# Late key steps, one VectorE order and two waits for constants moved in a three-stage transformer kernel

## The chip, the cores and the metric

The kernel runs on one core of one Trainium2 chip. Its time is the device time of one execution in microseconds (us); the kernel before took 1489.43 us (median of 3 runs, 1488.98 to 1492.85). One execution was profiled, and all rows below come from it.

## The reference

The input is 16 sequences (batches) of 256 tokens with 128 channels. The result is a chain of residual blocks, all in float32:

```python
x = x + 0.5 * channel_mix(layernorm(x))                 # L0 ffn
x = x + causal_attention(layernorm(x))                  # L0 attn, 16 heads of width 8
x = x + 0.5 * channel_mix(layernorm(x))
x = x + 0.5 * experts(layernorm(x))                     # L1 ffn: top 2 of 8 experts
x = x + focus_attention(layernorm(x))                   # L1 attn
x = x + 0.5 * experts(layernorm(x))
```

The focus attention is iterated three times over the same keys and values:

```python
q = (ln(x) @ Wq.T + bq) * sc                            # per head below
k, v = ln(ln(x)) @ Wk.T, ln(ln(x)) @ Wv.T + bv
for i in range(3):
    sq, sk = ln(q @ lq.T + lq_b), ln(k @ lk.T + lk_b)
    out = softmax(window(sq @ sk.T)) @ (v @ lv.T + lv_b)
    q = q + out                                         # unless converged
output = out @ Wo.T + bo
```

## The kernel before, in words

Every engine has its own program, written out by hand in the order in which it shall run; semaphores join the programs. The stages are: the causal stage with the channel mixes; the expert mixture by groups of two batches (`mixture`), some of it dense and some by sorted tiles; the focus stage (`fast_focus`, three iterations over 16 batches, so 48 rounds); the second expert mixture.

The keys, queries and values of the focus stage are made by group as well. For groups 0 to 4 this is done within the mixture; for groups 5, 6 and 7 it is put into the first 13 rounds of iteration 0 and called *late* (`late_keys`, `KEYS_LATE`). A late group takes five steps, 0 to 4, in five rounds in a row: rounds 0 to 4 for group 5, 4 to 8 for group 6, 8 to 12 for group 7. So rounds 1, 5, 9 have step 1; rounds 2, 6, 10 have step 2; rounds 3, 7, 11 have step 3; rounds 0, 4, 8 have step 0 and rounds 4, 8, 12 step 4.

A round on TensorE is eight turns hp = 0 to 7. Each starts with the scores of two heads (`pair_scores`, L2145; S0 to S7 below). Between them stand:

- `fast_values(n, p, g)` (L2156, V0 to V3): exponentials times values for four heads, V0 to V2 of the round itself, V3 of the round before;
- `back_tokens` (L1633, ps_m<-ident,o_sb; BT0 and BT1): the transposes of the last round's result, both into one half of `ps_m`. BT1 waits until VectorE has read BT0's result (`normalise`, L3131 and L3138);
- `front_tokens`, `front_product`, `front_heads` (FT; FP, L2128; FH, ps_m<-ident,y x2): the queries of the round after next;
- the late work, which uses the same half of `ps_m` as BT0 and BT1: `key_tokens` (KT, step 1, ps_m<-ident,y x4), products L2022 of `key_queries` and `key_keys` (step 2) and `key_values` (step 3), and `key_heads` (step 3). Before BT0 of a late round TensorE waits for semaphore `K_read` or `K_hi`, which says that VectorE has read the last product.

VectorE's round, as the code has it:

```python
front_tokens, evacuate_group(n - 1, 3), front_deviations      # L3096, L3119, L3026/L3029/L3032
normalise(n - 1, 0), evacuate_group(n, 0), normalise(n - 1, 1)
front_heads, change                                           # L2923/L2932, L3147
evacuate_group(n, 1), front_parts, evacuate_group(n, 2)       # L3119, L3111/L3112, L3119
```

`front_deviations` ends in `hvar` (L3032), from which ScalarE makes the scale of the queries. The late steps stand between these: `key_norm2` (four L2540, step 1; TensorE's `key_tokens` waits for it), `key_queries` (L2898, step 2) and `key_values` (L2913, step 3).

ScalarE does the exponentials (L1420), eight to a round. The operands `q_st` and `k_st` of round n are written by DMA during round n - 1, from the parts that `front_parts` and GpSimd made in round n - 2.

Between the causal stage and the mixture every engine jumps over a long branch that isn't taken (`redo_causal`). GpSimd then makes eight constants (L957 to L964 and a select, L773) for `positions` and `tile_experts`, which run in group 1 of the mixture, about 50 us later.

Of the kernel before, what the change touches and what calls it, by code (L numbers as in the profile page):

```python
# [17 lines left out]
B, T, C = 16, 256, 128  # L18
# [50 lines left out]
def macaron_kernel(nc, a, out):  # L69
    ctx = ExitStack()  # L70
    with ctx:
# [1557 lines left out]
        def _(pe):  # L1629
# [562 lines left out]
            def fast_focus():  # L2192

                last_group(lambda g, u: mixture(g, u, 0, True, True, more=lambda g, e: ahead(0, g, e)))
                for it in range(MAX_ITER):
                    final = it == MAX_ITER - 1

                    def body(n, b, p, half):
# [4 lines left out]
                        for hp in range(HP):  # L2203
                            pair_scores(n, p, half, hp)
                            for g, step in late:
                                if (step, hp) == (2, 1):
                                    key_queries(g)
                                if (step, hp) == (3, 1):
                                    key_values(g)
                            if hp == 0 and again:  # L2210
                                for t in range(NT):
                                    back_tokens(n - 1, B - 1, it - 1, t)
                            if hp == 1 and again:
                                pe.wait_ge(sem("fast_o_read"), (n - 1 + B) * NT + NT + 1)
                            if hp == 3 and again:
                                change_sum(it - 1, 1)
                                front_product(ahead[0])
                            if hp == 1 and final and isinstance(b, int) and b == B - 1:
                                mix_tokens(FIRST)
                            if hp == 1:  # L2220
                                if ahead:
                                    front_tokens(ahead[0])
                                if not first:
                                    fast_values(n - 1, 1 - p, NGV - 1)
                            elif hp == 2 and ahead and not again:
                                front_product(ahead[0])
                            elif hp == 3:
                                if first and not it:
                                    pe.wait_ge(sem("M_comb"), FIRST * EXP + QUADS + 2)
                                if late:  # L2230
                                    fast_values(n, p, 0)
                                for g, step in late:
                                    if step == 1:
                                        pe.wait_ge(sem("K_hi"), g + 1)
                                    if step == 2:
                                        pe.wait_ge(sem("K_read"), g * 3 + 1)
                                    if step == 3:
                                        pe.wait_ge(sem("K_read"), g * 3 + 3)
                                    if step == 4:
                                        pe.wait_ge(sem("K_hi"), g + 2)  # L2240
                                if not first:
                                    back_tokens(n - 1, b - 1, it, 0)
                                if not late:
                                    fast_values(n, p, 0)
                            elif hp == 4 and not first:
                                back_tokens(n - 1, b - 1, it, 1)
                            elif hp == 5:
                                fast_values(n, p, 1)
                            elif hp == 6:
                                if ahead:  # L2250
                                    front_heads(ahead[0])
                                for g, step in late:
                                    if step in (2, 3):
                                        pe.wait_ge(sem("fast_o_read"), (n - 1 + B) * NT + NT + 1)
                                    if step == 2:
                                        key_keys(g)
                                    if step == 3:
                                        key_heads(g)
                                if not first and final:
                                    back_out(b - 1)  # L2260
                                if final and isinstance(b, int) and b == B - 1:
                                    mix_logits(FIRST, 0)
                            elif hp == 7:
                                if not first and final:
                                    back_project(b - 1)
                                fast_values(n, p, 2)
                                for g, step in late:
                                    if step == 1:
                                        pe.wait_ge(sem("fast_o_read"), (n - 1 + B) * NT + NT + 1)
                                        key_tokens(g)  # L2270

                    fast_steps(pe, it, body)
                    n = it * B + B - 1
# [167 lines left out]
            def ahead(k, g, e):  # L2441
# [7 lines left out]
                if (g, e) == (0, 7):  # L2449
                    mix_logits(a + 1, 0)  # L2450
                if (g, e) == (1, 1):
                    pe.wait_ge(sem("consts"), CONSTS + 8)
                    positions(k)
                if (g, e) == (2, 6):
                    quad_rows(k, 0)
# [12 lines left out]
            def tiles(k):  # L2468
# [6 lines left out]
                for c in CHUNKS[k]:  # L2475
                    for i in range(SLOTS):
# [11 lines left out]
                            tile_hidden(c + 1, i + 3 - SLOTS)  # L2488
                        tile_out(c, i, at[order_in(c) * SLOTS + i])

            for g in range(AHEAD):
                mixture(g, g % 2, 0, True, more=lambda g, e: ahead(0, g, e))
            pe.wait_ge(sem("tile_in_0"), 16)
# [11 lines left out]
        def _(dve):  # L2505
# [664 lines left out]
            def fast_focus():  # L3170
# [3 lines left out]
                for it in range(MAX_ITER):  # L3174
                    final = it == MAX_ITER - 1

                    def body(n, b, p, half):
# [7 lines left out]
                            front_tokens(ahead[0])  # L3185
                        if not first:
                            evacuate_group(n - 1, NGV - 1)
                        for g, step in late:
                            if step == 2:
                                key_queries(g)  # L3190
                            if step == 3:
                                key_values(g)
                        if ahead:
                            front_deviations(ahead[0])
                        for g, step in late:
                            if step == 0:
                                key_stats1(g)
                        if not first:
                            normalise(n - 1, it, 0)
                        evacuate_group(n, 0)  # L3200
# [4 lines left out]
                            front_heads(ahead[0], it + 1 if later else it)  # L3205
                        if not first:
                            change(n - 1, b - 1, it)
                        for g, step in late:
                            if step == 1:
                                key_norm2(g)  # L3210
                        evacuate_group(n, 1)
                        if not first and final:
                            back_out(b - 1)
                        for g, step in late:
                            if step == 0:
                                key_norm1(g)
                        if ahead:
                            front_parts(ahead[0], p)
                        for g, step in late:
# [350 lines left out]
            def ahead(k, g, e):  # L3570
# [10 lines left out]
                if (g, e) == (0, 7):  # L3581
                    mix_ranks(a + 1)
                if (g, e) == (1, 1):
                    dve.wait_ge(sem("consts"), CONSTS + 8)
                    tile_experts(k)
                if (g, e) == (2, 5):
                    if k:
# [35 lines left out]
            def weigh_tiles(k):  # L3623
# [14 lines left out]
                quad_out(CHUNKS[k][-1], QUADS - 2)  # L3638
                quad_out(CHUNKS[k][-1], QUADS - 1)

            for g in range(AHEAD):
                mixture(g, g % 2, 0, True, more=lambda g, e: ahead(0, g, e))
            weigh_tiles(0)
# [44 lines left out]
```

## Time and profile before

| | before |
|---|---|
| median of 3 runs | 1489.43 us |
| the profiled execution | 1489.43 us, span 1487.7 us |
| TensorE busy, matmuls | 1326.3 us, 89% of the span |
| VectorE busy | 1008.0 us, 68% |
| ScalarE busy | 866.1 us, 58% |
| GpSimd busy | 529.1 us, 36% |
| mean granted TensorE clock | 0.967 of full speed |

Iteration 0 of the focus stage runs from 681.56 us (first exponential) to 884.43 us. In the rows, PE is TensorE, PEld its weight load, DVE VectorE, ACT ScalarE and POOL GpSimd. A fp32 matmul has two records, so an x16 in the trace is eight matmuls in the code.

### The profile page before, as it was taken

The numbers are of one execution on the slowest core, as the hardware profiler recorded it, in microseconds if no ns is written. First come the engines' busy times: TensorE is split into PE (matmuls) and PEld (weight loads), VectorE is DVE, ScalarE is ACT, GpSimd is POOL, SyncE is SP. The second block draws the span as 40 slices with busy tenths as digits, with TensorE's granted clock in tenths as the row PEclk, the third lists the DMA queues.
The fourth block names the chain that finished last, engine by engine and source line by source line (L and its number), as shares of the span: only waits on it lengthen the run. The fifth ranks groups of instructions, "written<-read, shape, count | busy, mean of one in ns | idle before, by whom it ended". The sixth has DMA issues, their size and how long they took to land. (4 is left out here: it accounts for less than half of the span.)

```text
span 1487.7 us, 36643 instructions
## 1 busy us (share of the span) xinstructions
PE 1326.3 (89%) x11651; PEld 919.3 (62%) x11651; DVE 1008.0 (68%) x3275; ACT 866.1 (58%) x1613; POOL 529.1 (36%) x818
## 2 busy tenths in 40 slices
PE   4799999998769999998889989999899999799998
PEld 2566666666546787775555545555555555567876
DVE  3688889888738755776676666665766666576544
ACT  3567777776424444435667767777666666333453
POOL 5366666665310503112323332333322222003444
PEclk9799999999869999999999999999999999999999
DMA  5332232233040112005454454455444443001232
GB/s 142 85 81 57 77 85 56 70 85 86 1 129 1 40 52 64 20 12 123 105 128 114 118 131 109 114 128 131 113 103 114 111 113 82 2 10 49 84 120 78
DMA packets 81070, 123.64 MB, mean 83 GB/s; under 512 B 10124, under 2 KB 64676, under 8 KB 71722
## 3 DMA queue, kind: packets, MB, share of 16 engines
q1 hardware_dynamic: 77866, 115.71, 30.5%
q0 software_dynamic: 3072, 6.30, 1.4%
q8 instruction: 68, 1.11, 0.3%
q14 instruction: 64, 0.52, 0.1%
HBM read 88.28 MB, written 33.56 MB: 82 GB/s over the span
## 5 line engine op out<-in xcount | busy, mean ns | idle before, releaser
L1420 ACT ACTIVATE e_buf<-ps_q 128x1024 f32<-128x1024 f32 x192 | 196.5, 1023 | 96.3 <-PE ps_q L2145 95.9
L2156 PE MATMUL ps_o<-e_buf,v_st 128*32 128x256 f32 x3072 | 210.0, 392 | 4.6 <-POOL v_st L1025 4.2
L1420 ACT ACTIVATE e_buf<-ps_k 128x1024 f32<-128x1024 f32 x192 | 195.7, 1019 | 20.3 <-PE ps_k L2145 18.2
L2006 PEld LDWEIGHTS ps_o<-w,e_buf 128*128 128x128 f32 x1280 | 152.4, 193 | 13.1 <-issue 12.0
L2006 PE MATMUL ps_o<-w,e_buf 128*128 128x128 f32 x1280 | 158.7, 278 | 0.0
L2594 DVE TENSOR_REDUCE mx<-ps_q 128x3 f32<-128x384 f32 x256 | 130.2, 548 | 27.4 <-PE ps_q L1710 26.8
L3119 DVE COPY o_sb<-ps_o 128x256 f32<-128x256 f32 x192 | 80.7, 421 | 100.2 <-PE ps_o L2156 60.7
L2145 PE MATMUL ps_q<-q_st,k_st 73*128 73x256 bf16 x768 | 119.6, 279 | 17.4 <-DMA q_st<-scr_q 15.4
L1237 ACT ACTIVATE e_buf<-ps_k 128x768 f32<-128x768 f32 x128 | 103.3, 807 | 47.9 <-PE ps_k L1721 45.9
L2156 PEld LDWEIGHTS ps_o<-e_buf,v_st 128*32 128x32 f32 x3072 | 81.3, 110 | 75.7 <-issue 36.4
L2145 PEld LDWEIGHTS ps_q<-q_st,k_st 73*128 73x128 bf16 x768 | 61.6, 99 | 97.7 <-issue 68.9
L2145 PE MATMUL ps_k<-q_st,k_st 73*128 73x256 bf16 x768 | 117.8, 276 | 1.9 <-ACT e_buf L1420 0.8
L886 POOL TENSOR_SCALAR_AFFINE_SELECT e_buf<-e_buf 128x512 f32<-128x512 f32 x128 | 85.5, 668 | 92.6 <-ACT e_buf L1237 91.0
L1336 ACT ACTIVATE e_buf<-ps_q,b_t 128x512 f32<-128x512 f32 x80 | 54.6, 685 | 93.3 <-PE ps_q L1998 89.6
L1336 ACT ACTIVATE e_buf<-ps_k,b_t 128x512 f32<-128x512 f32 x80 | 53.9, 685 | 71.9 <-PE ps_k L1998 68.7
L1633 PE MATMUL ps_m<-ident,o_sb 128*128 128x128 f32 x508 | 80.3, 281 | 12.9 <-DVE o_tok L3138 8.3
L2145 PEld LDWEIGHTS ps_k<-q_st,k_st 73*128 73x128 bf16 x768 | 72.8, 99 | 18.4 <-ACT e_buf L1420 10.3
L1047 POOL COPY heads_out<-o_tok 128x256 f32<-128x256 f32 (+1 forms) x32 | 12.9, 402 | 197.3 <-DVE dsum L3153 99.7
L1033 POOL TENSOR_TENSOR rest<-qk,parts 128x256 f32<-128x256 f32 x48 | 32.6, 680 | 139.1 <-DVE parts L3112 139.0
L1707 PE MATMUL ps_q<-mask_q,ident_b 128*128 128x256 bf16 x256 | 72.5, 283 | 9.5 <-DVEq L3415 4.5
L984 POOL DMA_INDIRECT slots_in<-heads_out,vp_all x40 | 39.3, 983 | 103.1 <-DVEq L3513 91.7
L1633 PEld LDWEIGHTS ps_m<-ident,o_sb 128*128 128x128 f32 x508 | 57.3, 142 | 30.0 <-DVE o_tok L3138 17.8
(403 smaller groups left out, 3068.0 us busy)
## 6 DMA issues: line engine op xcount, KB each, us to landing
q_st<-scr_q SPq DMA_DIRECT2D x64, 576.0 KB
k_st<-scr_k SPq DMA_DIRECT2D x192, 192.0 KB
scr_q<-parts SPq DMA_DIRECT2D x64, 192.0 KB, 2.1
scr_k<-parts SPq DMA_DIRECT2D x72, 64.0 KB
slots_in<-heads_out SPq DMA_DIRECT2D x3, 1536.0 KB
slots_out<-heads_out SPq DMA_DIRECT2D x18, 256.0 KB, 2.0
heads_out<-slots_in SPq DMA_DIRECT2D x15, 256.0 KB
out_dram<-x SPq DMA_DIRECT2D x8, 256.0 KB
```

The lines of the kernel that those rows point to most:

```text
L886: pool.affine_select(out=e, in_=e, compare_op=ALU.is_ge, fill=0.0, base=0, pattern=[[0, 2], [0, 2], [1, P]], channel_multiplier=-1)\
L984: pool.indirect_dma_start(slots_in[c], bass.IndirectOffsetOnAxis(ap=slot_no[c][:, k, t:t + 1], axis=0), normed_rows(ND + c * 2 + t // GT)[ ...
L1237: act.activation(e_buf[g % 2][:, hp * 2 % HG:hp * 2 % HG + 2, 0:3 * P], ps_k[:, :, 0:3 * P], ACT.Exp, bias=SHIFT).then_inc(sem("fast_exp"), 1)
L1336: act.activation(h_sb[e % 2][:, f, :], bank, ACT.Relu, bias=b1_t[:, j:j + 1])\
L1420: act.activation(e_buf[g % 2][:, hp * 2 % HG:hp * 2 % HG + 2, :], (ps_q, ps_k)[hp % 2][:, :, :], ACT.Exp).then_inc(sem("fast_exp"), 1)
L1633: return pe.transpose(dst, src, ident[0:k, 0:k])
L1707: mm(o[:, P:3 * P], ident_b[:, :], mask_q[:, :], start=True, stop=False, skip_group_check=True)
L2006: last = mm(ps_o[:, e % 2, t * P:(t + 1) * P], h_sb[e % 2][:, f, t * P:(t + 1) * P], w2[:, e * NF + f, :], start=f == 0, stop=f == NF - 1)
L2145: last = mm(bank[:, u, t * T:(t + 1) * T], k_st[p][0:ROWS_P1, hp * 2 + u, t * P:(t + 1) * P], q_st[p][0:ROWS_P1, hp * 2 + u, :], start=Tru ...
L2156: last = mm(ps_o[VW * j:VW * j + VW, g % 2, 0:T], v_st[p][:, kt, HG * g + j, :], e_buf[g % 2][:, j, kt * T:(kt + 1) * T], start=kt == 0, s ...
L2594: red(mx[:, h, :], ps_q[:, u, 0:3 * P].rearrange("p (c k) -> p c k", c=3), AX.X, ALU.max)\
L3119: dve.tensor_copy(o_sb[:, g, :], ps_o[:, g % 2, 0:T]).then_inc(sem("fast_evac"), 1)
```

## The change

There are four edits. On TensorE, in the 12 late rounds 1 to 12, V0 comes behind BT0 instead of ahead of it (so V0 comes behind the wait for `K_read` or `K_hi` too). On TensorE, `key_tokens` of step 1 moves from the end of the round (behind V2) to turn 6, ahead of S7 and V2. On VectorE, `key_queries` and `key_values` move behind `front_deviations`, and `key_norm2` behind the evacuation of V1. On TensorE and VectorE, the wait for the constants moves from group 1 of the mixture to the front of group 0. ScalarE, GpSimd and the DMA queue have the same program as before.

```diff
@@ TensorE, fast_focus
                             elif hp == 3:
                                 if first and not it:
                                     pe.wait_ge(sem("M_comb"), FIRST * EXP + QUADS + 2)
-                                if late:
-                                    fast_values(n, p, 0)
                                 for g, step in late:
...
                                 if not first:
                                     back_tokens(n - 1, b - 1, it, 0)
-                                if not late:
-                                    fast_values(n, p, 0)
+                                fast_values(n, p, 0)
...
                                 if ahead:
                                     front_heads(ahead[0])
                                 for g, step in late:
-                                    if step in (2, 3):
+                                    if step in (1, 2, 3):
                                         pe.wait_ge(sem("fast_o_read"), (n - 1 + B) * NT + NT + 1)
+                                    if step == 1:
+                                        key_tokens(g)
...
                                 fast_values(n, p, 2)
-                                for g, step in late:
-                                    if step == 1:
-                                        pe.wait_ge(sem("fast_o_read"), (n - 1 + B) * NT + NT + 1)
-                                        key_tokens(g)
@@ TensorE (VectorE alike, with tile_experts)
                 if (g, e) == (1, 1):
-                    pe.wait_ge(sem("consts"), CONSTS + 8)
                     positions(k)
...
+            pe.wait_ge(sem("consts"), CONSTS + 8)
             for g in range(AHEAD):
                 mixture(g, g % 2, 0, True, more=lambda g, e: ahead(0, g, e))
@@ VectorE, fast_focus
                             evacuate_group(n - 1, NGV - 1)
-                        for g, step in late:
-                            if step == 2:
-                                key_queries(g)
-                            if step == 3:
-                                key_values(g)
                         if ahead:
                             front_deviations(ahead[0])
                         for g, step in late:
                             if step == 0:
                                 key_stats1(g)
+                        for g, step in late:
+                            if step == 2:
+                                key_queries(g)
+                        for g, step in late:
+                            if step == 3:
+                                key_values(g)
...
                             change(n - 1, b - 1, it)
-                        for g, step in late:
-                            if step == 1:
-                                key_norm2(g)
                         evacuate_group(n, 1)
...
                         for g, step in late:
                             if step == 0:
                                 key_norm1(g)
+                        for g, step in late:
+                            if step == 1:
+                                key_norm2(g)
```

TensorE in round 1, from S6 to the first scores of round 2. Before, the transposes of `y` by four (KT) are the last of the round:

```order
L2145 MATMUL ps_q<-q_st,k_st 128x256 x4
L1633 MATMUL ps_m<-ident,y 128x128 x2
L2145 MATMUL ps_k<-q_st,k_st 128x256 x4
L2156 MATMUL ps_o<-e_buf,v_st 32x256 x8
L1633 MATMUL ps_m<-ident,y 128x128 x4
L2145 MATMUL ps_q<-q_st,k_st 128x256 x4
```

Now FH and KT stand together (two and four transposes, x6), ahead of S7 and V2:

```order
L2145 MATMUL ps_q<-q_st,k_st 128x256 x4
L1633 MATMUL ps_m<-ident,y 128x128 x6
L2145 MATMUL ps_k<-q_st,k_st 128x256 x4
L2156 MATMUL ps_o<-e_buf,v_st 32x256 x8
L2145 MATMUL ps_q<-q_st,k_st 128x256 x4
```

What moved is KT: S7 and V2 are now queued behind whatever KT waits for.

TensorE in round 2, from FP (L2128) to BT1. Before, V0 (L2156) follows S3:

```order
L2128 MATMUL ps_m<-block_w,y_t 128x128 x2
L2145 MATMUL ps_k<-q_st,k_st 128x256 x4
L2156 MATMUL ps_o<-e_buf,v_st 32x256 x8
L1633 MATMUL ps_m<-ident,o_sb 128x128 x4
L2145 MATMUL ps_q<-q_st,k_st 128x256 x4
L1633 MATMUL ps_m<-ident,o_sb 128x128 x4
```

Now BT0 (the first L1633) does:

```order
L2128 MATMUL ps_m<-block_w,y_t 128x128 x2
L2145 MATMUL ps_k<-q_st,k_st 128x256 x4
L1633 MATMUL ps_m<-ident,o_sb 128x128 x4
L2156 MATMUL ps_o<-e_buf,v_st 32x256 x8
L2145 MATMUL ps_q<-q_st,k_st 128x256 x4
L1633 MATMUL ps_m<-ident,o_sb 128x128 x4
```

V0 and BT0 have changed places, with BT0's wait for `K_read` now ahead of both.

VectorE in rounds 1 and 2, from `dsum` of round 1 to the reciprocal of round 2, before (the line numbers of VectorE are five higher here than in the changed kernel):

```order
L3147 TENSOR_REDUCE dsum<-o_tok 128x1
L2540 TENSOR_SCALAR y<-y,mv_k,rstd_k 128x128 x4
L3119 COPY o_sb<-ps_o 128x256
L3111 COPY qk<-ps_m 128x256
L3112 CAST parts<-ps_m 128x256
L3119 COPY o_sb<-ps_o 128x256
L3096 COPY y_t<-ps_m 128x256
L3119 COPY o_sb<-ps_o 128x256
L2898 SCALAR_TENSOR_TENSOR qcur<-ps_m,rows 128x512
L3026 TENSOR_TENSOR cen<-ps_m,rows 128x256
L3029 TENSOR_TENSOR sqr<-cen 128x256
L3032 TENSOR_REDUCE hvar<-sqr 128x32
```

and now:

```order
L3142 TENSOR_REDUCE dsum<-o_tok 128x1
L3114 COPY o_sb<-ps_o 128x256
L2535 TENSOR_SCALAR y<-y,mv_k,rstd_k 128x128 x4
L3106 COPY qk<-ps_m 128x256
L3107 CAST parts<-ps_m 128x256
L3114 COPY o_sb<-ps_o 128x256
L3091 COPY y_t<-ps_m 128x256
L3114 COPY o_sb<-ps_o 128x256
L3021 TENSOR_TENSOR cen<-ps_m,rows 128x256
L3024 TENSOR_TENSOR sqr<-cen 128x256
L3027 TENSOR_REDUCE hvar<-sqr 128x32
L2893 SCALAR_TENSOR_TENSOR qcur<-ps_m,rows 128x512
```

`key_norm2` (the four TENSOR_SCALAR) is behind the copy of V1, and `key_queries` (`qcur<-ps_m`) behind the three instructions that end in `hvar`. `key_values` moved in the same way in step 3.

## Rows read from the trace of the kernel before

**Rows 1.** The page, busy us, share of the span and instructions of each engine:

```profile
PE 1326.3 (89%) x11651; PEld 919.3 (62%) x11651; DVE 1008.0 (68%) x3275; ACT 866.1 (58%) x1613; POOL 529.1 (36%) x818
```

**Rows 2.** Waits of TensorE, 681 to 890 us: total us, times, longest:

```profile
PE ps_m L1633 <- DVE o_tok L3138: 6.3, 13, 1.3
PE ps_q L2145 <- DMA q_st<-scr_q: 5.8, 4, 2.9
```

**Rows 3.** Timeline of TensorE, round 14, not late (start, us, instruction [idle before]):

```profile
851.67 0.60 PE L2145 MATMUL ps_k<-q_st,k_st 73*128 73x256 bf16 x4
852.11 0.60 PE L1633 MATMUL ps_m<-ident,o_sb 128*128 128x128 f32 x4
...
854.09 0.60 PE L1633 MATMUL ps_m<-ident,o_sb 128*128 128x128 f32 x4
...
856.86 0.44 PE L1633 MATMUL ps_m<-ident,y 128*128 128x128 f32 x2
```

**Rows 4.** Timeline of TensorE: rounds 6 and 8 in one row each, round 9:

```profile
760.59 0.60 PE L2145 MATMUL ps_q<-q_st,k_st 73*128 73x256 bf16 x4 [0.97 <-DMA q_st<-scr_q]
...
794.45 0.65 PE L1633 MATMUL ps_m<-ident,o_sb 128*128 128x128 f32 x4 [1.32 <-DVE o_tok L3138]
...
802.53 0.60 PE L2145 MATMUL ps_k<-q_st,k_st 73*128 73x256 bf16 x4
...
805.50 0.66 PE L1633 MATMUL ps_m<-ident,o_sb 128*128 128x128 f32 x4 [0.34 <-DVE o_tok L3138]
...
808.32 0.44 PE L1633 MATMUL ps_m<-ident,y 128*128 128x128 f32 x2 [0.19 <-DVE y L2932]
...
810.22 0.63 PE L1633 MATMUL ps_m<-ident,y 128*128 128x128 f32 x4
811.09 0.60 PE L2145 MATMUL ps_q<-q_st,k_st 73*128 73x256 bf16 x4 [0.24 <-DMA q_st<-scr_q]
```

**Rows 5.** Timeline of VectorE, round 9:

```profile
808.43 1.68 DVE L2540 TENSOR_SCALAR y<-y,mv_k,rstd_k 128x128 f32<-128x128 f32 x4
810.04 0.41 DVE L3119 COPY o_sb<-ps_o 128x256 f32<-128x256 f32 x1
```

**Rows 6.** Timeline of TensorE, round 10:

```profile
815.06 0.60 PE L2145 MATMUL ps_k<-q_st,k_st 73*128 73x256 bf16 x4
...
816.59 0.66 PE L1633 MATMUL ps_m<-ident,o_sb 128*128 128x128 f32 x4
...
818.02 0.66 PE L1633 MATMUL ps_m<-ident,o_sb 128*128 128x128 f32 x4 [0.34 <-DVE o_tok L3138]
```

**Rows 7.** Timeline of VectorE, round 10:

```profile
814.75 0.68 DVE L2898 SCALAR_TENSOR_TENSOR qcur<-ps_m,rows 128x512 f32<-128x512 f32 x1
815.35 0.41 DVE L3026 TENSOR_TENSOR cen<-ps_m,rows 128x256 f32<-128x256 f32 x1
...
816.37 0.42 DVE L3032 TENSOR_REDUCE hvar<-sqr 128x32 f32<-128x256 f32 x1
```

**Rows 8.** Timeline of TensorE, round 11:

```profile
829.31 0.71 PE L2128 MATMUL ps_m<-block_w,y_t 128*128 128x128 f32 x4 [0.78 <-DVE y_t L3096]
829.86 0.60 PE L2145 MATMUL ps_k<-q_st,k_st 73*128 73x256 bf16 x4
...
832.82 0.66 PE L1633 MATMUL ps_m<-ident,o_sb 128*128 128x128 f32 x4 [0.34 <-DVE o_tok L3138]
```

**Rows 9.** Timelines of TensorE, GpSimd and VectorE where the mixture starts:

```profile
425.33 2.08 PE L1998 MATMUL ps_q<-z_t,w 128*128 128x512 f32 x2 [3.46 <-issue]
...
426.85 0.29 POOL L773 TENSOR_SCALAR_AFFINE_SELECT k_const<-k_const 128x128 bf16<-128x128 bf16 x1
...
427.89 0.87 DVE L2531 BATCH_NORM_STATS2 st<-x 128x6 f32<-128x128 f32 x4 [4.76 <-issue]
...
428.44 2.08 PE L1998 MATMUL ps_q<-z_t,w 128*128 128x512 f32 x2 [1.04 <-ACT e_buf L1336]
```

**Rows 10.** Windows in round 3: length, busy us (x) by engine, PEclk, DMA:

```profile
727.00:730.40 3.40, 3.40 (x25) 1.65 (x23) 1.15 (x3) 1.37 (x3) 0.00 (x0) 0.51 0.60 135
```

More of the change, by code:

```diff
@@ L3583, in ahead @@
                 if (g, e) == (1, 1):
-                    dve.wait_ge(sem("consts"), CONSTS + 8)
                     tile_experts(k)
@@ L3639, in weigh_tiles @@
                 quad_out(CHUNKS[k][-1], QUADS - 1)
+            dve.wait_ge(sem("consts"), CONSTS + 8)
             for g in range(AHEAD):
```

## The prediction

> **What bounds the kernel now.** I read the page's engine line first: TensorE's matmuls are busy 89% of the span and no other engine is over 68% [rows 1], so wherever TensorE stops, the stop shows in the time unless something behind it waits anyway. Then the waits of TensorE over iteration 0 of the focus stage: 13 waits for `o_tok` (6.3 us) and 4 for the query operands (5.8 us) [rows 2]. Last the timelines, round by round. In a round that isn't late, S3 starts at 851.67, BT0 at 852.11, BT1 at 854.09 without a wait, FH at 856.86 [rows 3]: BT0 comes 0.44 behind S3, BT1 2.42 behind S3 (1.98 behind BT0, since V0 and S4 lie between), FH 2.77 behind BT1. In late round 9 V0 lies ahead of BT0, so only S4 lies between BT0 and BT1, and BT1 waits 0.34 for VectorE: S3 to BT1 is 2.97, to FH 5.79 instead of 5.19 [rows 3, 4]. TensorE is the pace of a late round, and VectorE is the engine that it waits for. Times below are starts.
>
> **V0 behind BT0, taken alone.** It gives a late round the order of rows 3: BT1 0.55 earlier. That holds only where VectorE has by then read the late product and `normalise` isn't held up. In rounds 4 and 8 BT1 waits 1.32 for `o_tok` [rows 4], because VectorE does `key_stats1` ahead of `normalise`; VectorE's own chain sets BT1 and the new order gives nothing. Round 0 has no BT0. In round 12 up to 0.6 could be won, but round 14 waits for its query operands (the second of the four waits in size, 5.8 - 2.9 - 0.97 - 0.24 = 1.7 [rows 2, 4]), which I expect to swallow it: 0, with -0.6 as the other end.
>
> **Step 1 (rounds 1, 5, 9): KT ahead of S7 and V2.** KT needs `key_norm2`, which is now behind VectorE's copy of V1. In round 9 as it was: BT1 805.50, `key_norm2` 808.43 to 810.11 (2.93 behind BT1), the copy behind it 0.41, KT 810.22 [rows 4, 5]. Now BT1 is at 802.53 + 2.42 = 804.95; the copy comes first, at 807.88, `key_norm2` starts about 0.35 later, 808.25, lasts 1.68, KT at 810.04. TensorE is free for it behind FH, at 807.72 + 0.3 = 808.0, so it stands still for 2.0, and S7 and V2 stand behind it. Before, S7 and V2 ran in that time: from FH to KT is 1.90, less 0.3 for FH itself 1.6, of which I take 1.5 for the two. KT itself takes 0.46 before the next may start. So the next S0 is at 810.04 + 0.46 + 1.5 = 812.0, against 811.09: +0.9. In round 10 a wait of 0.24 for `q_st` was swallowed on the way, in round 6 one of 0.97 [rows 4], in round 2 none: +0.9, +0.2 and +1.2, together **+2.3**. The ends: 0 if `key_norm2` ran before FH, which no row speaks for, and 3 x 2.0 = 6.0 if the whole standstill counts.
>
> The 1.68 are four operations of 128 columns in fp32, SBUF to SBUF, at a time when GpSimd copies and adds. Of that the Trainium skill ("GPSIMD Engine Reference", Key points) says that GpSimd shares its SBUF interfaces with VectorE, so that they contend. By that rule the 0.35 of delay would move `key_norm2` partly out of GpSimd's way and step 1 would cost some tenths less; the sum stays with the measured 1.68.
>
> **Step 2 (rounds 2, 6, 10): BT0 waits for `key_queries`, which is now behind `hvar`.** As it was: `key_queries` 814.75 to 815.43, over before TensorE had finished V0; BT0 816.59 [rows 6, 7]. Now `cen` takes its place; it needs FP and can start between 814.75 and 815.35, I take 815.25. `hvar` starts 1.02 later [rows 7], 816.27, `key_queries` 0.33 behind it, 816.6, and ends at 817.28; BT0 at 817.34. V0 is queued behind BT0, so nothing covers the wait of 817.34 - (815.06 + 0.44) = 1.84. BT1 follows 1.98 later, 819.32, against 818.02: **+1.3** in each, **+3.9**. From BT1 to the end of the round the order is as it was, and VectorE's and ScalarE's work for the next round hangs on the same TensorE instructions, so all of it shifts.
>
> **Step 3 (rounds 3, 7, 11): the same with `key_values`.** FP at 829.31 lasts 0.71; `cen` can start at 829.95, `hvar` at 830.97, `key_values` (128x512 as in rows 7, 0.68) ends at 831.98, BT0 at 832.04, BT1 834.02 against 832.82 [rows 8]: **+1.2** each, **+3.6**. Both ends for steps 2 and 3: -0.55 each if VectorE's read were over in time (the pure gain of the order), and +1.8 each if no part of V0 covered.
>
> **The wait for the constants.** GpSimd's last constant ends at 427.14, TensorE's first product of the mixture started at 425.33 and VectorE's first operation at 427.89 [rows 9]. VectorE loses nothing. TensorE starts up to 1.9 later; but its second product stood back by 1.04, and both gaps are of issue and not of data that the mixture needs, so that the later start may close one: between +0.8 and +1.9, I take **+1.0**. The wait that goes from group 1 was long met there: 0.
>
> **The clock.** Sum so far 2.3 + 3.9 + 3.6 + 1.0 = 10.8. In round 3, behind waits of which none is over 0.78 (round 11 has the same, [rows 8]), the granted clock is 0.51, the lower level of 1.2 GHz, for 3.4 us with TensorE busy all the time [rows 10]: up to 1.7 lost. Rounds 7 and 11 have the same waits and keep 2.4 GHz. The nine longer standstills give such falls more places. I put one more of them, **+1.5**, into the sum; the ends are -1.7 (the one in round 3 goes) and three or four more.
> The Trainium skill ("TensorE: Matmul & The Clock Gate", A second HAM failure mode: psum-queue depth-cycling) says that frequent short idles between groups of matmuls are enough to make the clock swing between its two levels. By that rule this change, which adds such idles, costs more than their length; the fall in round 3 agrees, rounds 7 and 11 show that it isn't certain.
>
> **Sum.** +12.3 on a profiled execution of 1489.43, which is also the median: **1501.7**. No later stage has a fixed time that could take the delay up; all the rest is queued behind TensorE.
>
> **Rivals.**
> *The clock falls in most of the standstills (slower still).* In five of the nine: 10.8 + 5 x 1.6 = 18.8, 1508.2. For it: round 3. Against it: the waits of 1.32 in rounds 4 and 8 [rows 4] had no such fall. The page's rule above would make this the likely case.
> *The new order wins (faster).* The mechanism is the earlier BT0: if VectorE's read of the late product ends before S3 + 0.44 in steps 2 and 3, and `key_norm2` before FH in step 1, ten rounds win 0.55 each, with +1.0 for the constants: -4.5, 1484.9. It decides at 815.5 in round 10; I have the read ending at 817.28 there. For it speaks only that rounds 13 to 15 run so.
> *No change.* The round is set by the query operands, and the standstills only replace waits for them. All four such waits are 5.8, of them the largest 2.9, and 0.97 and 0.24 are in the sum [rows 2, 4]; the remaining 1.7 is that of round 14, behind the late rounds. If VectorE's read comes about 1 earlier than I have it (`key_queries` in the gap ahead of `cen`), steps 2 and 3 come out near +0.3 and the total near +2: 1491.5.
>
> **How the numbers follow.** Forecast (10.8 with none to two more falls of the clock) 0.66, with a range of its own from 1496 to 1505; clock rival 0.13, no change 0.12, faster 0.09. A difference under 0.3% (4.5 us) can't be told from none here. Faster than 1485.0: 0.08; within: 0.13; slower than 1493.9: 0.79. The range that leaves out 2 in 10: 1493 to 1508.
>
> **What would show it.** In the changed kernel's timeline of TensorE: KT waits about 2.0 for `y` (L2535) in rounds 1, 5 and 9; BT0 waits about 1.8 for `qcur` in rounds 2, 6, 10 and about 1.7 for `vp_all` in rounds 3, 7, 11 (S3 to BT0 2.2 to 2.3); rounds 4 and 8 keep the wait of 1.3 for `o_tok`; S3 to BT1 in round 12 is 2.4. The first product of the mixture starts behind the last constant. Rounds of iterations 1 and 2 keep their lengths. I am wrong if BT0 shows no wait in steps 2 and 3, if the start of the focus stage moves by more than 2 us, or if rounds 1 to 12 together grow by less than 6 us.

## The result: 1.45% slower, and the profile after

| | before | after |
|---|---|---|
| median | 1489.2 us (4 runs, 1487.99 to 1492.85) | 1510.01 us (4 runs, 1505.88 to 1515.52) |
| ratio | | 1.0145, 95% interval 1.0116 to 1.0175 |
| span of the profiled execution | 1487.7 us | 1508.3 us |
| first exponential of the focus stage | 681.56 | 681.56 |
| iteration 0 of the focus stage | 202.9 us | 223.8 us |
| iteration 1 | 184.1 us | 183.9 us |

The forecast was 1501.7 with a range to 1508: the side was right, the size short by 8.3 us, and the time lies above the range. All of the loss is in iteration 0. The page's engine line after, beside [rows 1]:

```profile
PE 1336.4 (89%) x11651; PEld 927.8 (62%) x11651; DVE 1009.1 (67%) x3275; ACT 865.0 (57%) x1613; POOL 528.6 (35%) x818
```

No instruction was added, yet the matmuls are busy for 10.1 us more. That is the first hint: waiting alone would leave the busy time as it was.

The length of a round, from one first exponential (L1420) to the next, in both traces:

| round | step | before | after | grown by | I had |
|---|---|---|---|---|---|
| 1, 5, 9 | 1 | 13.50, 12.71, 12.00 | 14.74, 12.79, 12.78 | 2.1 | 2.3 |
| 2, 6, 10 | 2 | 15.16, 15.08, 15.08 | 16.41, 16.40, 16.40 | 3.9 | 3.9 |
| 3, 7, 11 | 3 | 13.51, 12.02, 12.01 | 17.22, 17.32, 17.39 | 14.4 | 3.6 |
| 4, 8 | 4 and 0 | 11.40, 11.40 | 11.40, 11.39 | 0.0 | 0 |
| 12 | 4 | 10.41 | 10.18 | -0.2 | 0 |
| 0, 13 | 0, none | 13.44, 11.90 | 13.85, 12.32 | 0.8 | 0 |

The waits of TensorE from 681 to 905 us after, the counterpart of [rows 2]:

```profile
PE ps_q L2145 <- DMA q_st<-scr_q: 5.4, 2, 3.3
PE ps_m L1633 <- DVE vp_all L2908: 5.1, 3, 1.7
PE ps_m L1633 <- issue: 5.1, 3, 1.7
PE ps_m L1633 <- DVE qcur L2893: 5.1, 3, 1.7
...
PE ps_m L1633 <- DVE o_tok L3133: 2.7, 2, 1.4
```

Each of the three predicted standstills is there three times, 1.7 long: `vp_all` is BT0 in step 3, `qcur` BT0 in step 2, and "issue" KT in step 1 (the view names no engine; KT starts 0.10 behind the end of VectorE's four instructions). The thirteen waits for `o_tok` have become two, those of rounds 4 and 8.

Step 1, TensorE in round 9 after, the counterpart of [rows 4]; then VectorE, of [rows 5]:

```profile
815.82 0.60 PE L2145 MATMUL ps_k<-q_st,k_st 73*128 73x256 bf16 x4
816.26 0.60 PE L1633 MATMUL ps_m<-ident,o_sb 128*128 128x128 f32 x4
...
818.24 0.60 PE L1633 MATMUL ps_m<-ident,o_sb 128*128 128x128 f32 x4
...
821.01 0.44 PE L1633 MATMUL ps_m<-ident,y 128*128 128x128 f32 x2
823.15 0.63 PE L1633 MATMUL ps_m<-ident,y 128*128 128x128 f32 x4 [1.70 <-issue]
```

```profile
821.12 0.42 DVE L3114 COPY o_sb<-ps_o 128x256 f32<-128x256 f32 x1
821.45 1.60 DVE L2535 TENSOR_SCALAR y<-y,mv_k,rstd_k 128x128 f32<-128x128 f32 x4
```

S3 to BT0 0.44, to BT1 2.42, to FH 5.19, as in a round that isn't late; then KT stands until `key_norm2` ends at 823.05.

Step 3, TensorE in round 11 after, the counterpart of [rows 8]:

```profile
844.71 0.71 PE L2128 MATMUL ps_m<-block_w,y_t 128*128 128x128 f32 x4 [0.77 <-DVE y_t L3091]
845.26 0.60 PE L2145 MATMUL ps_k<-q_st,k_st 73*128 73x256 bf16 x4
847.56 1.11 PE L1633 MATMUL ps_m<-ident,o_sb 128*128 128x128 f32 x4 [1.70 <-DVE vp_all L2908]
848.61 1.94 PE L2156 MATMUL ps_o<-e_buf,v_st 128*32 128x256 f32 x16
...
851.30 1.06 PE L1633 MATMUL ps_m<-ident,o_sb 128*128 128x128 f32 x4
...
853.14 1.94 PE L2156 MATMUL ps_o<-e_buf,v_st 128*32 128x256 f32 x16
...
857.67 1.07 PE L2156 MATMUL ps_o<-e_buf,v_st 128*32 128x256 f32 x16
```

The wait is what I had. What I had not is behind it: V0 and V1 take 1.94 instead of the 1.07 of V2. The windows say why (length, busy us and count of PE, PEld, DVE, ACT, POOL, then the granted clock, the DMA share and GB/s):

```profile
843.80:847.20 3.40, 1.28 (x10) 0.83 (x8) 2.74 (x9) 1.52 (x3) 0.00 (x0) 0.96 0.72 181
847.20:850.60 3.40, 3.04 (x21) 1.44 (x22) 0.85 (x3) 1.14 (x2) 0.00 (x0) 0.50 0.05 14
850.60:854.00 3.40, 3.40 (x20) 2.16 (x22) 1.44 (x5) 1.77 (x2) 0.00 (x0) 0.50 0.02 5
854.00:857.40 3.40, 3.40 (x25) 2.31 (x18) 1.89 (x6) 1.30 (x2) 1.08 (x2) 0.54 0.00 0
857.40:860.80 3.40, 3.40 (x46) 1.84 (x43) 0.86 (x3) 3.02 (x5) 2.68 (x4) 1.00 0.08 26
```

In the first window TensorE is busy for only 1.28 of 3.4 us. At its end, at 846.9, the clock falls to its lower level, 1.2 GHz, and it stays there for 10.2 us although TensorE is busy for nearly all of that time. Rounds 3 and 7 show the same, so rounds 2 to 11 have 30.7 us at the lower level. Before, they had 3.4 us, in round 3 [rows 10]. (A further fall of 6.8 us, across rounds 0 and 1, is in both traces.)

The start of the mixture after, the counterpart of [rows 9], TensorE and GpSimd:

```profile
426.30 0.29 POOL L773 TENSOR_SCALAR_AFFINE_SELECT k_const<-k_const 128x128 bf16<-128x128 bf16 x1
426.64 3.78 PE L1998 MATMUL ps_q<-z_t,w 128*128 128x512 f32 x4 [5.32 <-POOL k_const L773]
430.21 2.01 PE L1998 MATMUL ps_k<-z_t,w 128*128 128x512 f32 x4
432.07 0.60 PE L1633 MATMUL ps_m<-ident,rank 128*8 128x128 f32 x4
```

The first product waits for the last constant, but the gap of 1.04 ahead of the second is gone, and the focus stage starts at the same 681.56. That equality is partly chance: the changed kernel came to the constants 0.55 earlier (426.30 against 426.85), and its first `ps_m<-ident,rank` 1.50 earlier (432.07 against 433.57), since the clock rose at 430.5 instead of 433.4; by the start of the focus stage this was used up again, in a stretch where the change only takes out a wait that was long met.

### The profile page after: what moved, and what is told of

It is laid out like the page before. It is cut to its first block and busy times, and to the rows that moved or that the text cites. A ratio compares the mean times of both kernels' runs of the same rounds, so it can differ in the third digit from the quotient of the medians.

```text
span 1508.3 us, 36640 instructions
## 1 busy us (share of the span) xinstructions
PE 1336.4 (89%) x11651; PEld 927.8 (62%) x11651; DVE 1009.1 (67%) x3275; ACT 865.0 (57%) x1613; POOL 528.6 (35%) x818
## 5 line engine op out<-in xcount | busy, mean ns | idle before, releaser
L1420 ACT ACTIVATE e_buf<-ps_q 128x1024 f32<-128x1024 f32 x192 | 196.3, 1022 | 110.7 <-PE ps_q L2145 110.0
L2156 PE MATMUL ps_o<-e_buf,v_st 128*32 128x256 f32 x3072 | 214.8, 399 | 4.6 <-POOL v_st L1025 4.2
L1420 ACT ACTIVATE e_buf<-ps_k 128x1024 f32<-128x1024 f32 x192 | 195.6, 1019 | 28.2 <-PE ps_k L2145 27.3
L2145 PE MATMUL ps_q<-q_st,k_st 73*128 73x256 bf16 x768 | 122.1, 283 | 14.7 <-DMA q_st<-scr_q 12.6
L2156 PEld LDWEIGHTS ps_o<-e_buf,v_st 128*32 128x32 f32 x3072 | 82.4, 112 | 78.0 <-issue 38.9
L1633 PE MATMUL ps_m<-ident,o_sb 128*128 128x128 f32 x508 | 82.5, 287 | 19.7 <-DVE o_tok L3133 5.2
L1047 POOL COPY heads_out<-o_tok 128x256 f32<-128x256 f32 (+1 forms) x32 | 12.8, 400 | 209.9 <-DVE dsum L3142 108.5
L1633 PEld LDWEIGHTS ps_m<-ident,o_sb 128*128 128x128 f32 x508 | 60.2, 146 | 31.0 <-DVE o_tok L3133 12.2
```

What stands on the lines that cost most here:

```text
L1420: act.activation(e_buf[g % 2][:, hp * 2 % HG:hp * 2 % HG + 2, :], (ps_q, ps_k)[hp % 2][:, :, :], ACT.Exp).then_inc(sem("fast_exp"), 1)
L1633: return pe.transpose(dst, src, ident[0:k, 0:k])
L2145: last = mm(bank[:, u, t * T:(t + 1) * T], k_st[p][0:ROWS_P1, hp * 2 + u, t * P:(t + 1) * P], q_st[p][0:ROWS_P1, hp * 2 + u, :], start=Tru ...
L2156: last = mm(ps_o[VW * j:VW * j + VW, g % 2, 0:T], v_st[p][:, kt, HG * g + j, :], e_buf[g % 2][:, j, kt * T:(kt + 1) * T], start=kt == 0, s ...
```

## The experiments

The theory, "stall and clock": most of the loss comes from the granted clock, which falls because TensorE stands still ahead of BT0; two edits must come together for it, VectorE's read put late and V0 no longer covering it. The rivals: V0's place alone; VectorE's order alone; KT; the constants; or another cause of slow step-3 rounds, such as the operands' DMA.

These runs were made in three groups on three other chips, on which the kernel before takes 1565.1 (`before_again`, `after_again`, `fill3`, `fill23`), 1560.6 (`v0_only`, `keys23`, `step1`, `values_back`) and 1561.4 us (the other four). So one more execution of the kernel before was traced, on the first of these chips:

> The kernel before once more, for its trace on the chip of these runs. Iteration 0 of the focus stage as in the first trace, 203 us; whatever the whole time is there, the difference lies outside of it.

It took 1563.0 us, with iteration 0 at 201.6 us against 202.9 in the first trace. Its rounds 3, 7 and 11 took 12.0 each and hold no fall of the clock: the fall in [rows 10] did not come back. The extra time is mostly in the second expert mixture, its windows first in the first trace, then in `before_again`:

```profile
1280.00:1487.00 207.00, 195.36 (x1261) 151.51 (x1259) 118.15 (x469) 87.69 (x199) 61.34 (x64) 0.99 0.20 61
```

```profile
1297.00:1561.00 264.00, 212.69 (x1262) 164.16 (x1260) 117.34 (x470) 87.26 (x200) 60.99 (x64) 0.89 0.16 48
```

The change doesn't touch that stage. I compare ratios to the kernel before on the same chip, and the lengths of rounds.

| run | what differs | ratio to before, 95% interval | iteration 0 |
|---|---|---|---|
| before_again | nothing | | 201.6 us |
| after_again | full change | 1.0106 (1.0055 to 1.0157) | 225.1 |
| v0_only | V0 behind BT0 | 0.9999 (0.9971 to 1.0027) | 203.5 |
| dve_only | VectorE's key reads late | 1.0034 (1.0011 to 1.0058) | 209.7 |
| keys23 | both | 1.0104 (1.0075 to 1.0134) | not used |
| step1 | KT and key_norm2 | 1.0023 (0.9998 to 1.0048) | 207.8 |
| consts | the two waits | 1.0014 (0.9995 to 1.0033) | 205.8 |
| values_back | full, key_values back | 1.0064 (1.0033 to 1.0094) | 214.8 |
| keys_back | full, both reads back | 1.0018 (0.9995 to 1.0040) | 205.7 |
| fill3 | full, wait filled in step 3 | 1.0128 (1.0083 to 1.0174) | 222.5 |
| fill23 | full, filled in steps 2 and 3 | 1.0065 (1.0044 to 1.0087) | 214.0 |
| early | another order of the late chain | 0.9984 (0.9969 to 1.0000) | 202.9 |

The ratios are the estimates on record, with their intervals; the plain ratio of two medians comes out up to 0.0025 higher (1.0131 for `after_again`).

**v0_only.**

```diff
-                                if late:
-                                    fast_values(n, p, 0)
...
-                                if not late:
-                                    fast_values(n, p, 0)
+                                fast_values(n, p, 0)
```

> The kernel before with one edit: V0 behind BT0 in the late rounds; VectorE's order, KT and the constants as before. Theory 'stall and clock' (the loss of the full change comes from BT0 waiting for a VectorE read that is now late, and from the granted clock that falls behind that wait): here VectorE's read is over in time, BT0 has no wait, BT1 loses its 0.34, about 0.55 us is won in each of eight rounds (1 to 3, 6, 7, 10 to 12), no new fall of the clock: 1484 to 1486 us. Rival 'V0 is the cover' (moving V0 alone exposes BT0): rounds 2, 3, 6, 7, 10, 11 are longer by 1 us or more each, 1495 us or more.

Rounds 3, 7, 11 took 11.4 us (12.0 in `before_again`), rounds 2 and 10 14.6 and 14.5 (15.2 and 15.1): the 0.6 is there. But round 6 took 16.1 (15.1) and round 0 14.7 (13.5), so rounds 0 to 11 together win only 1.9 us (154.3 against 156.2), and rounds 12 to 15 lose 3.7 (49.2 against 45.4), in this one trace. On the whole V0's place alone neither costs nor wins anything that can be measured. The rival is refuted, but so is my "no new fall of the clock" and the win of 3 to 5 us: rounds 6 and 8 hold a fall of 3.4 us each and rounds 13 and 14 one of 6.8 us, and the one in round 8 follows the old wait of 1.36 for `o_tok`.

**keys23.** Both halves: the diff above and, on VectorE,

```diff
-                            if step == 2:
-                                key_queries(g)
-                            if step == 3:
-                                key_values(g)
                         if ahead:
                             front_deviations(ahead[0])
...
+                            if step == 2:
+                                key_queries(g)
+                            if step == 3:
+                                key_values(g)
```

> The kernel before with V0 behind BT0 and with key_queries and key_values behind front_deviations; KT, key_norm2 and the constants as before. 'Stall and clock': step-2 rounds +1.3 us each, step-3 rounds +3.7 to +5.4 each (1.2 of wait, the rest half clock), other late rounds up to 0.55 less: 1505 to 1508 us. Rival 'the falls of the clock need the whole change' (KT ahead of S7, or the shifted start): step-3 rounds only +1.2, 1495 to 1497 us.

1.0104 is 16 us; the full change has 1.0145 on the first chip and 1.0106 on another. So the two edits on BT0 are enough for all of it, as far as these intervals tell. The execution that was profiled took 1589.0 us, well above the median of 1578.4, so its trace isn't read.

**dve_only.** VectorE's part of the diff alone.

> The kernel before with key_queries and key_values behind front_deviations and nothing else. V0 is still ahead of BT0 and covers 1.0 of the wait: BT0 stands still 0.7 instead of 1.7, +0.7 us in each of six rounds, 4 us in all, ratio 1.002 to 1.004, if such short waits leave the clock up. If VectorE's order alone is the cause: falls of the clock as in the full change, ratio 1.008 or more.

+5 us, against 0 for V0's place alone and 16 for both: together they cost far more than their sum. The waits of TensorE:

```profile
PE ps_m L1633 <- DVE qcur L2898: 2.1, 3, 0.7
...
PE ps_m L1633 <- DVE vp_all L2913: 0.7, 1, 0.7
```

Where V0 stands ahead of BT0 the wait is 0.7 instead of 1.7. Rounds 2, 6 and 10 took 15.9 us (15.1 or 15.2 in `before_again`), which is about that wait; rounds 3, 7 and 11 took 13.6, 13.2 and 12.8 (12.0), and the first two of these hold a fall of 3.4 us each.

**step1.** KT and `key_norm2` as in the change.

> The kernel before with KT at turn 6 and key_norm2 behind the copy of V1; all else as before. Both theories: KT waits about 2 us for key_norm2 in rounds 1, 5, 9; +1.3, +0.2, +0.9 us as in the full change and up to 0.55 more in each, because V0 is still ahead of BT0: 1491 to 1494 us. If waits of 2 us by themselves bring the clock down, each costs 1.5 to 4 us more: 1496 us or more.

1.0023, 3.6 us, as expected, though the interval just reaches 1. KT's wait is there three times (the "issue" row). Rounds 9 and 10 (14.4 and 15.7) hold a fall of the clock of about 3.4 us between them; rounds 5 to 8 hold none. So a wait of 1.7 here does not bring the clock down every time.

```profile
PE ps_m L1633 <- issue: 5.1, 3, 1.7
```

**values_back.** The full change with `key_values` ahead of `front_deviations` again.

> The changed kernel with key_values alone back ahead of front_deviations. 'Stall and clock': step-3 rounds lose both the wait of 1.7 and the fall of the clock and are as short as or shorter than before (12.0 us), step-2 rounds stay at 16.4: 1492 to 1495 us. Rival 'the clock falls because of the wait in the step-2 round ahead': step-3 rounds stay at 16 us or more, 1503 us or more.

Step-3 rounds fell to 11.41 us each, so the wait and all of the half clock are gone from them with the one edit undone, and that rival is refuted. But the time isn't at 1.003: step-2 rounds now took 17.97, 17.96 and 18.03, 1.6 longer than the 16.4 of the full change's first trace, with the clock down for 3.4 us in each. Rounds 4 and 8 took 12.61 instead of 11.40, each with a fall of 3.4 us behind its wait of 1.35 for `o_tok`.

**keys_back.** Both reads back, the other edits kept.

> The changed kernel with both key_queries and key_values back ahead of front_deviations; V0 behind BT0, KT at turn 6 and the constants stay changed. 'Stall and clock': BT0 has no wait in steps 2 and 3, no fall of the clock in those rounds (14.6 and 11.4 us); what is left is KT's wait, about +2 us, less some 0.55 per round: ratio to before 0.998 to 1.002. Rival (something else in the change costs): 1.004 or more.

1.0018 against the full change's 1.0106 (on another chip): what is left can't be told from nothing. Steps 2 and 3 are shorter than before, 14.53 and 11.4 us; KT's wait, a fall of the clock in round 1 (16.5 us) and one in each of rounds 4 and 8 (12.62 us instead of 11.40) take it back. The loss is made by the two late reads together with V0's place.

**after_again, fill3, fill23.** The test of the clock itself. In `fill3` TensorE computes V0 once more in the wait, without a signal:

```diff
+                                if [g for g, step in late if step in (3,)]:
+                                    values_idle(n, p, 0)      # V0's products, without then_inc
                                 for g, step in late:
                                     if step == 1:
                                         pe.wait_ge(sem("K_hi"), g + 1)
```

> The changed kernel once more, beside the two with filling. Ratio to before 1.012 to 1.016; step-3 rounds of 16 to 17.5 us, with the granted clock at half for 7 to 10 us in each.

> The changed kernel; in rounds 3, 7 and 11 TensorE computes V0 once more (the same eight heads' products, without a signal) in the wait ahead of BT0, so that 1.0 of the 1.7 us of standstill is filled and BT0 starts when it did. More work, no wait shorter by it. 'Stall and clock': the clock stays up in these rounds, they take 13.2 us instead of 17.3, the time falls by 9 to 12 us, ratio to before 1.006 to 1.009. Rival 'the rounds are slow for another reason (operands by DMA, the longer chain of VectorE)': as the changed kernel or slower, ratio 1.012 or more.

> As before it, with the second V0 in rounds 2, 6 and 10 too. In the first trace of the changed kernel step-2 rounds had no fall of the clock (16.4 us), so 'stall and clock' expects the same time as with filling in step 3 alone, or up to 5 us less where the clock falls in step-2 rounds; ratio 1.004 to 1.009. Rival: 1.012 or more.

`after_again` misses what I expected of it. The ratio is 1.0106, below my 1.012 to 1.016, though its interval reaches over it; the step-3 rounds take 14.9 us, with 3.4 us at the lower clock in each instead of 7 to 10. In its place falls stand all over the late rounds. Of the nine standstills of 1.70, eight have one at their end or within 1.0 us behind it, and so has the wait of 1.36 in round 4, whose fall lasts 6.8 us (round 4 took 13.9 us instead of 11.4). Rounds 2 to 11 have 34.1 us at the lower level, where the first trace of the change has 30.7. This is TensorE in round 5, behind KT's standstill, and the window there:

```profile
785.00 0.63 PE L1633 MATMUL ps_m<-ident,y 128*128 128x128 f32 x4 [1.70 <-issue]
785.47 0.89 PE L2145 MATMUL ps_k<-q_st,k_st 73*128 73x256 bf16 x4
786.29 1.94 PE L2156 MATMUL ps_o<-e_buf,v_st 128*32 128x256 f32 x16
```

```profile
785.60:789.00 3.40, 3.40 (x26) 1.43 (x24) 0.42 (x1) 1.51 (x2) 1.73 (x3) 0.51 0.10 31
```

TensorE in round 11 of `fill3` (L2167 is the filling):

```profile
868.82 0.71 PE L2128 MATMUL ps_m<-block_w,y_t 128*128 128x128 f32 x4 [0.78 <-DVE y_t L3104]
869.37 0.60 PE L2145 MATMUL ps_k<-q_st,k_st 73*128 73x256 bf16 x4
869.90 1.07 PE L2167 MATMUL ps_o<-e_buf,v_st 128*32 128x256 f32 x16
871.68 0.66 PE L1633 MATMUL ps_m<-ident,o_sb 128*128 128x128 f32 x4 [0.70 <-DVE vp_all L2921]
872.26 1.07 PE L2156 MATMUL ps_o<-e_buf,v_st 128*32 128x256 f32 x16
```

```profile
869.80:873.20 3.40, 2.70 (x38) 1.25 (x36) 2.19 (x6) 1.37 (x3) 0.00 (x0) 1.00 0.40 104
```

BT0 starts 2.31 behind S3, as after the change (2.30), so nothing waits less; but V0 takes 1.07 and the granted clock is 1.00. The step-3 rounds are 13.33, 13.33 and 13.34 us, my 13.2, against 17.2 to 17.4 in the first trace and 14.9 in `after_again`. The whole time did not fall: 1.0128 meets the condition that I had written down for the rival, and by the ratio alone the rival would have it. The rounds decide otherwise, since those that were filled are free of falls. Here the full change has falls in all late steps, those of step 2 among them (18.0, 17.8, 18.0), and `fill3` leaves these (18.0, 19.4, 17.8) and adds one in round 1 (16.5 against 14.0). `fill23` fills step 2 too: step-2 rounds 16.41, 16.41 and 16.41, step-3 rounds 13.33, 14.10 and 14.07 (rounds 7 and 11 keep a fall of 3.4 us each), iteration 0 11.1 us shorter than in `after_again`, and 6.8 us at the lower level in rounds 2 to 11 instead of 34.1. Its ratio is 1.0065. The interval overlaps that of the full change (from 1.0055), but the runs hardly do: 10 of `fill23` from 1572.7 to 1580.8 us, median 1576.9, and 4 of the full change from 1580.3 to 1589.5, median 1585.6. More work, BT0 no earlier, and the kernel is 8.7 us faster: that is the clock's share, as far as the filling reaches.

The windows of iteration 0, `after_again` and then `fill23`:

```profile
700.00:926.20 226.20, 192.66 (x1886) 116.22 (x1886) 135.42 (x407) 139.62 (x189) 70.45 (x124) 0.92 0.42 106
```

```profile
700.00:915.00 215.00, 189.39 (x1984) 114.76 (x1983) 134.31 (x404) 139.76 (x190) 70.47 (x124) 0.96 0.45 111
```

98 more matmul records, and 3.3 us less of busy time.

**consts.** The two waits alone.

> The kernel before with only the two waits for the constants at the front of the mixture. My sum had +1.0 us. The trace of the changed kernel has the focus stage starting when it did before, so: ratio 0.999 to 1.001, first product of the mixture right behind the last constant. Rival (the wait delays the whole mixture by its 1.9 us, and something else hid it): 1.001 to 1.002 and the focus stage 1 to 2 us later.

Unclear: 1.0014, interval from 0.9995. In its trace the first `ps_m<-ident,rank` starts 6.75 behind the last constant's start, 6.59 in `before_again`; whatever the wait costs at that place is 0.2 us. The focus stage starts at 699.73, 1.2 later than in `before_again` (698.54), which is what the rival had; but in the traces of this section it starts anywhere from 694.8 to 703.3, so that 1.2 shows nothing. Whether there is anything more in the 1.0014 the runs don't say.

**early.** What the experiments pointed to: TensorE's waits in the late rounds are worth more than their length, so take some away. From the kernel before:

```diff
-                                if (step, hp) == (2, 7):      # ScalarE
+                                if (step, hp) == (3, 1):
                                     key_heads(g)
@@ VectorE
+                        if ahead and not (first and it):
+                            front_tokens(ahead[0])
                         for g, step in late:
                             if step == 3:
                                 key_heads(g)
-                        if ahead and not (first and it):
-                            front_tokens(ahead[0])
```

> The kernel before with two moves of its own: ScalarE's key_heads from behind the eighth exponential of the step-2 round to behind the second of the step-3 round, and VectorE's front_tokens ahead of key_heads in step 3, so that exponential 0, S2 and FP of rounds 3, 7, 11 don't wait for the late key chain. If TensorE's waits set the rounds: each of the three about 1.2 us shorter (10.8 instead of 12.0), the falls of the clock there less likely, ratio 0.996 to 0.999. Rival: the saving is swallowed by waits for the operands two rounds on: 0.999 to 1.001.

0.9984 with an interval that ends at 1.0000: 1559.6 against 1561.4 us. The step-3 rounds did not become 10.8: they took 13.6, 15.2 and 13.6 (12.0 in `before_again`), and it is the step-2 rounds that are shorter, 12.5 instead of 15.1. Rounds 2 and 3 together are 26.2 us (27.2 in `before_again`), 10 and 11 26.1 (27.1), 6 and 7, with a fall of 3.4 us, 27.7 (27.1). If it wins, it wins 2 us; iteration 0 of its trace is no shorter. It has the lowest median of its group, and not clearly so.

## Why the prediction was right or wrong

**Right: the waits and their places.** I had KT at S3 + 7.51 (810.04 - 802.53); it came at S3 + 7.33. I had BT0's standstill at 1.84 in step 2 and 1.74 in step 3; the trace prints 1.70 for both, measured from the end of S3. Step 2 grew by 3.9 as forecast to the tenth. Step 1 grew by 2.1 (2.3). Rounds 4 and 8 kept their length and their wait for `o_tok`. The waiting part of step 3 is 13.33 - 12.02 = 1.31 a round, by `fill3`, 3.9 in all (3.6).

**Wrong: the term "the clock".** I put one more fall, +1.5, into the sum, with "three or four more" as the end. The step-3 rounds grew by 14.4, of which 3.9 is waiting: 10.5 is the clock, half of the whole loss and seven times the term (the rounds lose 11.9 to it, and lost 1.5 before, in round 3). With the fall of [rows 10] and one more, I had 6.8 us at the lower level in rounds 2 to 11; the traces of the change show 30.7 and 34.1. Two things were mis-sized.

First the length. I priced a fall by the one in [rows 10], 3.4 us and at most 1.7 lost. In the first trace of the change each of the three lasts 10.2 us and costs 3.9 to 4.1 (17.2 to 17.4, less 13.3).

Second the chance. I took one of the nine standstills; three brought the clock down in the first trace, and eight of nine in `after_again`. I argued from the waits of 1.32 in rounds 4 and 8, which had no fall, and from rounds 7 and 11. That was the record of one execution in the old order, and in the new order it does not hold. Over the traces that are read here, the 12 waits of 1.3 in rounds 4 and 8 with V0 ahead of BT0 have no fall at or behind them, but six of 14 have one where V0 is behind BT0. Of the standstills of 1.70 in steps 1 and 2, which stand alone, 18 of 33 have one (from none of six in the first trace to five of six in `after_again`). Those of step 3, where 0.28, 0.67 and 0.77 stand just ahead of the 1.70, have it in six of six. What decides it for a standstill that stands alone, these traces don't show.

With the clock at what it measured, my sum would be 1489.4 + 10.8 + 10.5 = 1510.7, against 1510.0. That it comes so near is partly luck: it still holds +1.0 for the constants, which the trace doesn't show, and lacks the 0.8 by which rounds 0 and 13 grew.

The rival "the clock falls in most of the standstills" had 1508.2 with a chance of 0.13; it was nearest, and it should have been the forecast. The time lies above even this rival's because it, too, priced a fall at 1.6. The Trainium skill ("TensorE: Matmul & The Clock Gate", A second HAM failure mode: psum-queue depth-cycling) tells of a kernel whose frequent short idles between groups of matmuls made the clock swing between its two levels. The traces agree with it: 30.7 and 34.1 us at the lower level behind idles of no more than 1.7 us.

**Wrong, small: the constants.** +1.0 forecast, 0.0 found at the start of the focus stage, 0.2 at its own place in `consts`. The lower end (0.8) was too high there, since the gap of 1.04 went and the clock rose earlier, not later. What the wait costs over the whole kernel stays open: `consts` allows for -0.8 to +5.2 us.

**Wrong, small: round 12.** I had S3 to BT1 at 2.4; it is 2.65 (861.77 to 864.42). The round is 0.2 shorter all the same.

**Not decided.** Whether VectorE's `key_norm2` gains from moving away from GpSimd's work. It took 1.60 in all traces of kernels where it is moved and 1.68 or 1.69 in the others, 0.08 less a round. But it has hardly moved away: GpSimd is busy beside it for 1.00 us instead of 1.09.

## What to carry to other kernels

Price a new wait on TensorE with the lower clock that may follow it: here that cost up to three times the wait (4.1 against 1.3 us a round). It followed in all six cases where a wait of 1.7 joined other short ones and in about half of those where it stood alone, and matmuls that nobody needed were cheaper than standing still. Don't take the number of falls from one trace; two executions of one kernel had them in different rounds. Work that covers a wait and the order that shortens it belong together; taken apart, one of the two edits here cost 0 and the other 5 us, together 16. When a busy time grows and no instruction was added, look at the granted clock before any chain of waits.

## What the runs showed of the hardware that I had not expected

The granted clock stayed at half for 10.2 us with TensorE busy in all of the last two thirds, while a fall at [rows 10] ended after 3.4 us. Where the falls lie differs between two executions of one kernel: in the first trace of the change those of rounds 2 to 11 were all in step 3 (three of 10.2 us, none in steps 1 and 2), in `after_again` every step-2 and every step-3 round has one of 3.4 us (1.3 to 1.6 us lost), and so have rounds 5 and 9, beside the one of 6.8 us behind the wait of round 4. The kernel before took 1489 us in one place and 1563 in the trace of the other; of these 74 us, 57 are in the second mixture, where the granted clock is 0.89 against 0.99 and the same number of matmuls is busy for 212.7 against 195.4 us. Of the 57 us that explains 17; the other 40 are idle time of TensorE, whose cause no run here shows.
